# Laying the causal mask from ScalarE instead of multiplying it in, in a macaron layer with an mLSTM core

## The chip, the cores and the metric

The kernel runs on one core of one Trainium2 chip. The metric is the device time of one execution in microseconds (us); the time of the kernel before is the median of three runs.

## What is computed

The layer adds three things to an input of 4 sequences of 512 tokens by 128 channels: half of a top-1 mixture of experts (8 experts, 128 to 512 to 128), then an mLSTM block, then half of the same mixture again. The part that matters here is the mLSTM block. Its recurrence

```python
m_t = jnp.maximum(ft + m, it)
ie = jnp.exp(it - m_t)
fe = jnp.exp(ft - m_t + m)
c = fe[..., None, None] * c + ie[..., None, None] * jnp.einsum('bhd,bhe->bhde', vt, kt)
n = fe[..., None] * n + ie[..., None] * kt
num = jnp.einsum('bhde,bhe->bhd', c, qt)
den = jnp.maximum(jnp.sum(n * qt, -1, keepdims=True), 1.0)
```

over 512 steps and 8 heads of 64 is computed in chunks of 128 tokens. Inside a chunk the output is a masked product: scores (k times q, 128 by 128 for each head) are multiplied by decays exp(a_s - m_t) where s <= t, and by 0 elsewhere. What comes from before the chunk is the running state times q, scaled by a state decay exp(min - m_t). The zeros of the causal mask are made by adding -1e30 ahead of the exponential.

## The kernel before

Each engine has its own program, written out by hand, and semaphores tie them together. The mixture of experts runs first (`ffn(0)`), then four sequences (`sequence(b, last)`, three as iterations of a loop and the last unrolled), then `ffn(1)`. A sequence is four chunks (`chunk(b, c, last)`, c = 0 to 3). While the chunks of a sequence run, the projections of what comes next are woven in. After chunk 3 stand the q and k projections of the next sequence.

The eight banks of PSUM (the accumulator memory, 128 partitions by 512 fp32 each) have fixed uses. `PJ` is two banks, used in turn by the projections v, o, r (gate) and s (skip), so that each projection waits for the reader of the one two before it: project s waits for `take(.., "o")`, project r for `take(.., "v")`. `TR` holds transposes and state updates. `SB` is two banks for the scores of the even and of the odd heads. `NB_` is two banks for outputs. `DM` is one bank for the decays, used in a fixed order (`DM_USES`): carry and columns once for a sequence, then for every chunk even, odd and state. Each use waits until the use before it has been read (`dm_free`).

For a chunk TensorE does, in this order: decays of the even heads into DM, scores, project v of the next chunk, decays odd into DM, project o, a transpose of keys, state decays into DM, project r, project s, `from_state` (needs QS, the queries scaled by state decays), `to_state`, `values`. A group of decays is one identity matmul that writes the mask over the whole bank (128x512), and four 128x128 products accumulated on it. State decays have no mask.

ScalarE reads each group with four exponentials: `decays` (L796, even and odd, into DT, which shares its memory with the tile that the profile calls WVT), `state_decays` (L805, into E1, called E in the profile). Its order in a chunk is: decays even, `out_t` in chunk 3, take v, `out_t` in chunk 2 and `squares` in chunk 1, decays odd, `squares` in chunks 2 and 3, take o, state decays, take r, take s. VectorE multiplies scores by decays (`weigh`, L1994), makes QS from E1 (`scale_q`, L2001) and, after that, the chunk's head norm: `centre` ends in L2044, whose result `squares` (L816) reads.

In the profile every matmul but a few transposes is at L918, the helper, with "bank" as output: MASKB,IDB is the mask, M,SELQ a group of decays or state decays, SKIPB,ONESR the start of project s, CS,QS `from_state`. The timeline merges equal instructions (x4). For half of the 32 mask matmuls, those that open an even group, only the weight load is recorded and not the matmul.

Of the kernel before, what the change touches and what calls it, by code (L numbers as in the profile page):

```python
# [21 lines left out]
ACT = mybir.ActivationFunctionType  # L22
AX_X = mybir.AxisListType.X

P = 128
# [3 lines left out]
NC = 4  # L29
# [12 lines left out]
HD = 64  # L42
# [61 lines left out]
def macaron(nc, x, consts, colpack, rowpack, w_router, w1, w2, b2, wul, wult, wurt, wqt, wkt, wskt, wvt, wot,  # L104
# [9 lines left out]
    with ExitStack() as ctx:  # L114
        def sb(name, shape, dt=F32):
            return ctx.enter_context(nc.sbuf_tensor(name, shape, dt))

        def sem(name):
            return ctx.enter_context(nc.semaphore(name))
# [48 lines left out]
        IDB = sb("IDB", [P, P], BF16)  # L168
        MASKB = sb("MASKB", [P, 512], BF16)
# [3 lines left out]
        SELQ = sb("SELQ", [P, NC, H * P], BF16)  # L173
# [65 lines left out]
        M3 = sb("M3", [P, P], BF16)  # L239
# [12 lines left out]
        MINB = sb("MINB", [P, NC, NP_])  # L252
        E1 = sb("E1", [P, NP_, P])
# [75 lines left out]
        dm_full, dm_free, st_full, pt_ready = sem("dm_full"), sem("dm_free"), sem("st_full"), sem("pt_ready")  # L329
        hv_full, hv_read, cs_ready, qs_ready = sem("hv_full"), sem("hv_read"), sem("cs_ready"), sem("qs_ready")  # L330
        cen_ready, sq_ready, hvar_ready = sem("cen_ready"), sem("sq_ready"), sem("hvar_ready")
        hn_ready, outg_ready = sem("hn_ready"), sem("outg_ready")
        cs_copied = sem("cs_copied")


        PJ = bank[0:2]
        TR, DM = bank[2], bank[3]
        SB = bank[4:6]
# [26 lines left out]
            return pj_free[pj_bank(use)], b * (NPJ // 2) + pj_uses(b).index(use) // 2 + 2  # L365


        DM_USES = ["carry", "columns", *(f"{what}{c}" for c in range(NC) for what in ("even", "odd", "state"))]
        NDM = len(DM_USES)

        def dm_full_at(b, use):
            return dm_full, b * NDM + DM_USES.index(use) + 1

        def dm_read_at(b, use):
            return dm_free, b * NDM + DM_USES.index(use) + 2

# [229 lines left out]
        def _(act):  # L606
            a = nc.scalar
# [3 lines left out]
            def xn_channels(f, q):  # L611
                if f == 0:
                    act.wait_ge(xt_full[f], q + 1)
                    done = xt_copied[f]
                elif q < 3:
                    act.wait_ge(*pj_full_at(NB - 1, f"xt{q}"))
                    done = pj_free[q % 2]
                else:
                    act.wait_ge(xt_full[f], 1)
                    done = xt_copied[f]  # L620
                a.activation(XNT[:, q, :], bank[q % 2][:, :], ACT.Copy).then_inc(done, 1)
# [120 lines left out]
            def round_xc(b):  # L742

                act.wait_ge(xc_ready, b + 2)
                a.activation(XCH[:, :, :], XC[:, :, :], ACT.Copy).then_inc(xc_high, 1)
# [42 lines left out]
            def decays(b, c, hf):  # L788

                n = b * NC + c  # L790

                act.wait_ge(pt_ready, 2 * n + 1)
                act.wait_ge(*dm_full_at(b, f"{('even', 'odd')[hf]}{c}"))
                for m in range(4):
                    h = 2 * m + hf
                    ins = a.activation(DT[:, hf, m, :], DM[:, m * P:(m + 1) * P], ACT.Exp, bias=AC[:, c, h:h + 1])  # L796
                ins.then_inc(dm_free, 1)

            def state_decays(b, c):

                n = b * NC + c
                act.wait_ge(qs_ready, n + 1)
                act.wait_ge(*dm_full_at(b, f"state{c}"))
                for m in range(4):
                    ins = a.activation(E1[:, m, :], DM[:, m * P:(m + 1) * P], ACT.Exp, bias=MINB[:, c, m:m + 1])  # L805
                ins.then_inc(dm_free, 1)

            def first_state(b):

# [4 lines left out]
            def squares(b, c):  # L814
                act.wait_ge(cen_ready, b * NC + c + 1)
                a.activation(SQ[:, :, :], H2[:, :, :], ACT.Square).then_inc(sq_ready, 1)  # L816

            def out_t(b, c):

                act.wait_ge(*tr_full_at(b, f"o{c}"))  # L820
                a.activation(OUTT[:, :, :].rearrange("p m t -> p (m t)"), TR[:, :], ACT.Copy, scale=0.5)\
                    .then_inc(tr_free, 1)

            def chunk(b, c, last):
                nxt = (b, c + 1) if c < NC - 1 else None if last else (b + 1, 0)
                if c:
                    decays(b, c, 0)
                if c == 3:
                    out_t(b, 1)
                if last and c == 3:  # L830
                    xn_channels(1, 2)
                if nxt:
                    take(*nxt, "v")
                if c == 2:
                    out_t(b, 0)
                if c == 1:
                    squares(b, 0)
                decays(b, c, 1)
                if c > 1:
                    squares(b, c - 1)  # L840
                if nxt:
                    take(*nxt, "o")
                state_decays(b, c)
                if c == NC - 1 and not last:
                    round_xc(b + 1)
                    head_gates(b + 1)
                if nxt:
                    take(*nxt, "r")
                if c < NC - 1:
                    take(*nxt, "s")  # L850
                elif last:
                    layer_norm(1, 0)
                if c == 0:
                    first_state(b)
                if last and c == 2:
                    xn_channels(1, 0)
                    xn_channels(1, 1)
                if c == 1 and not last:
                    z_scaled(b + 1)
                if c == 2 and not last:  # L860
                    head_in(b + 1)
                    head_silu(b + 1)
# [51 lines left out]
        def _(pe):  # L914
            t_ = nc.tensor

            def mm(o, l, r, start=True, stop=True):
                return t_.matmul(o, l, r, start=start, stop=stop, skip_group_check=True)  # L918
# [178 lines left out]
            def dm_wait(b, use):  # L1097

                pe.wait_ge(dm_free, b * NDM + DM_USES.index(use) + 1)
                return DM  # L1100
# [106 lines left out]
            def decays(b, c, hf):  # L1207

                dm_wait(b, f"{('even', 'odd')[hf]}{c}")
                mm(DM[:, :], IDB[:, :], MASKB[:, :], True, False)  # L1210
                for m in range(4):
                    h = 2 * m + hf
                    ins = mm(DM[:, m * P:(m + 1) * P], SELQ[:, c, h * P:(h + 1) * P], M3[:, :], False, m == 3)
                ins.then_inc(dm_full, 1)

            def state_decays(b, c):

                dm_wait(b, f"state{c}")
                for m in range(4):

                    ins = mm(DM[:, m * P:(m + 1) * P], SELQ[:, c, 2 * m * P + HD:2 * m * P + HD + P], M3[:, :])
                ins.then_inc(dm_full, 1)

            def scores(b, c):

# [190 lines left out]
        def _(dve):  # L1416
# [580 lines left out]
            def scale_q(b, c):  # L1997

                n = b * NC + c
                dve.wait_ge(*dm_read_at(b, f"state{c}"))  # L2000
                v.tensor_tensor(QS[:, :, :], QT[:, :, c * P:(c + 1) * P], E1[:, :, :], ALU.mult).then_inc(qs_ready, 1)  # L2001

            def new_state(b, c):
# [279 lines left out]
```

## Time and profile before

| | |
|---|---|
| median of 3 runs | 427.73 us (426.88 to 428.43) |
| the profiled execution, its own time | 427.93 us |
| its span, first to last instruction | 425.7 us |
| mean granted TensorE clock | 0.953 of full speed; 1.00 from 125.5 to 345 us |
| sequence loop, one iteration | 57.7 us, from 125.5 us on |
| TensorE busy in the span | 378.5 us (89%) |
| VectorE busy | 320.2 us (75%) |
| ScalarE busy | 230.5 us (54%) |

The span lies 2.2 us below the execution's own time; that rest is start and end. Times in the rows are counted from the first instruction. "Busy" of TensorE counts pipelined matmuls, so 9 tenths busy can still hide waits of some tenths of a microsecond.

### The profile page before, as it was taken

How to read it: one execution, taken by the hardware profiler on the slowest of the kernel's cores; microseconds unless marked ns; L12 is line 12 of the kernel's file. 1: busy time of each engine (PE TensorE's matmuls, PEld its weight loads, DVE VectorE, ACT ScalarE, POOL GpSimd, SP SyncE). 2: the span in 40 equal slices, each digit the busy share in tenths (PEclk: the TensorE clock that was granted, in tenths of full speed). 3: DMA queues.
4: the chain of work that ended last, by engine and by line, in shares of the span. 5: the costliest groups of instructions: out<-in, count | busy, mean ns of one | idle time of the engine just before them, and what ended most of it. 6: DMA issues, size and time to landing. Idle time of an engine off the chain costs nothing.

```text
span 425.7 us, 11362 instructions
## 1 busy us (share of the span) xinstructions
PE 378.5 (89%) x3607; PEld 300.8 (71%) x3629; DVE 320.2 (75%) x1042; ACT 230.5 (54%) x607; POOL 124.2 (29%) x125
## 2 busy tenths in 40 slices
PE   8149999999999999999999999999989868779990
PEld 5123799964687777877878878778768734579990
DVE  4892677766728898878989788988788995567870
ACT  3641344442556767567684567665556912555550
POOL 5475145531001111103110121111031068434552
PEclk9657999999999999999999999999999969899997
DMA  6997122219999999989600000000001612323320
GB/s 199 370 418 227 46 78 62 68 57 217 181 171 174 174 170 162 175 170 173 153 5 0 0 0 0 0 0 0 2 2 42 235 62 87 113 82 92 97 68 0
DMA packets 57265, 46.10 MB, mean 108 GB/s; under 512 B 4112, under 2 KB 53906, under 8 KB 56722
## 3 DMA queue, kind: packets, MB, share of 16 engines
q1 hardware_dynamic: 53618, 37.84, 42.0%
q0 software_dynamic: 2752, 5.73, 3.9%
q10 hardware_dynamic: 864, 2.15, 1.6%
q8 instruction: 16, 0.26, 0.3%
q14 instruction: 15, 0.11, 0.1%
HBM read 17.99 MB, written 27.25 MB: 106 GB/s over the span
## 4 chain that ended last, share of the span: by engine, by line
PE 63%; DVE 12%; ACT 8%; issue 6%; DMA 3%; POOL 3%; another core or an unknown queue 1%; SPq 0%; DVEq 0%; POOLq 0%; ACTq 0%
PE bank L918 59%; ACT WVT L796 4%; POOL slots L521 2%; DVE ST L1450 1%; PE bank L1288 1%; ACT E L805 1%; PE bank L1055 1%; DMA XN<-slots 1%; ACT W1R L816 1%; DMA slots<-XN,POS 1%; DVE QS L2001 1%; ACT XNT L736 1%; DMA QKT<-by_token 1%; DMA by_token<-YB,IDX 1%
## 5 line engine op out<-in xcount | busy, mean ns | idle before, releaser
L569 POOL TENSOR_TENSOR HS<-HS,MHALF 128x8 f32<-128x8 f32 x16 | 26.4, 1647 | 130.9 <-DVE HS L2051 130.9
L918 PE MATMUL bank<-XBT,W1R 128*128 128x128 f32 x368 | 50.1, 280 | 0.5 <-ACT XBT L691 0.4
L918 PE MATMUL bank<-W,HT 128*128 x368 | 49.0, 276 | 0.7 <-issue 0.7
L918 PEld LDWEIGHTS bank<-XBT,W1R 128*128 128x128 f32 x368 | 45.3, 194 | 1.7 <-ACT XBT L691 1.4
L918 PEld LDWEIGHTS bank<-W,HT 128*128 128x128 f32 x368 | 44.8, 192 | 1.2 <-issue 0.8
L698 ACT ACTIVATE HT<-bank,W1R 128x128 f32<-128x128 f32 x115 | 34.8, 366 | 16.2 <-PE bank L918 12.5
L796 ACT ACTIVATE WVT<-bank,AC 128x128 f32<-128x128 f32 x128 | 36.6, 376 | 11.8 <-PE bank L918 11.7
L521 POOL DMA_INDIRECT slots<-XN,POS x32 | 32.6, 1018 | 19.4 <-issue 13.0
L918 PE MATMUL bank<-MASKB,IDB 128*128 128x512 bf16 x130 | 35.4, 398 | 3.0 <-POOL HS L569 1.2
L760 ACT ACTIVATE QKT<-bank,COLS 128x512 f32<-128x512 f32 x32 | 22.0, 687 | 29.0 <-PE bank L918 29.0
L550 POOL DMA_INDIRECT by_token<-YB,IDX x23 | 22.0, 958 | 30.3 <-DVE YB L1713 29.9
L553 POOL DMA_INDIRECT out<-YB,IDX x23 | 22.7, 985 | 24.4 <-DVE YB L1716 16.8
L918 PEld LDWEIGHTS bank<-MASKB,IDB 128*128 128x128 bf16 x151 | 14.5, 101 | 20.8 <-issue 3.3
L1994 DVE TENSOR_TENSOR WOT<-bank,WVT 128x512 f32<-128x512 f32 x32 | 21.9, 685 | 8.8 <-ACT WVT L796 8.5
L1706 DVE TENSOR_SCALAR HT<-bank,W1R 128x128 f32<-128x128 f32 x69 | 22.0, 347 | 8.4 <-PE bank L918 6.5
L691 ACT ACTIVATE XBT<-bank 128x128 f32<-128x128 f32 x46 | 12.6, 277 | 26.8 <-PE bank L1055 13.4
L1679 DVE COPY OUT<-B 128x128 f32 x41 | 10.3, 251 | 20.5 <-issue 17.5
L561 POOL TENSOR_TENSOR LA<-LA,MHALF 128x4 f32<-128x4 f32 x4 | 4.1, 1015 | 68.1 <-DVE LA L1869 68.1
L918 PE MATMUL bank<-M,SELQ 128*128 128x128 bf16 x192 | 18.7, 220 | 5.7 <-ACT WVT L796 3.3
L918 PEld LDWEIGHTS bank<-M,SELQ 128*128 128x128 bf16 x192 | 13.8, 98 | 10.2 <-ACT WVT L796 6.1
L1680 DVE COPY W1R<-W 128x516 f32 x41 | 18.7, 455 | 0.3 <-issue 0.3
L918 PE MATMUL bank<-QKT 64*128 64x128 f32 x256 | 18.6, 285 | 0.0
(363 smaller groups left out, 972.4 us busy)
## 6 DMA issues: line engine op xcount, KB each, us to landing
slots<-FILL SPq DMA_DIRECT2D x74, 258.0 KB, 7.9
W<-w SPq DMA_DIRECT2D x2, 2048.0 KB, 10.6
XN<-slots SPq DMA_DIRECT2D x23, 129.0 KB
W<-w SPq DMA_DIRECT2D x1, 2064.0 KB
slots<-QKT SPq DMA_DIRECT2D x1, 1483.5 KB, 6.2
XB<-slots SPq DMA_DIRECT2D x23, 64.5 KB
X<-x SPq DMA_DIRECT2D x4, 256.0 KB, 5.3
QKT<-by_token SPq DMA_DIRECT2D x4, 256.0 KB, 4.0
```

The costliest lines, as they stand in the source:

```text
L521: g.indirect_dma_start(out=slots[f], out_offset=bass.IndirectOffsetOnAxis(ap=POS[:, t:t + 1], axis=0), in_=XN[f][:, t, :], in_offset=None) ...
L550: ins = g.indirect_dma_start(out=by_token, out_offset=number, in_=YB[:, j, :], in_offset=None)
L553: ins = g.indirect_dma_start(out=out, out_offset=number, in_=YB[:, j, :], in_offset=None, bounds_check=NT * P - 1, oob_is_err=False)
L569: g.tensor_tensor(HS[:, 3, :], HS[:, 2, :], MHALF[:, 0:H], ALU.pow).then_inc(roots_ready, 1)
L691: a.activation(XBT[:, j % 2, :], bank[j % 2][:, 0:P], ACT.Copy).then_inc(xbt_copied[f], 1)
L698: ins = a.activation(HT[:, j % 2, c, :], bank[2 + j % 2][:, c * P:(c + 1) * P], ACT.Relu, bias=W1R[:, j % 2, F + c:F + c + 1])
L760: a.activation(QKT[:, m, :], PJ[i][:, :], ACT.Identity, bias=col("bq", m)).then_inc(pj_free[i], 1)
L796: ins = a.activation(DT[:, hf, m, :], DM[:, m * P:(m + 1) * P], ACT.Exp, bias=AC[:, c, h:h + 1])
L918: return t_.matmul(o, l, r, start=start, stop=stop, skip_group_check=True)
L1680: v.tensor_copy(W1R[:, j % 2, :], W1[:, e, :]).then_inc(w1_copied[f], 1)
L1706: ins = v.tensor_scalar(HT[:, j % 2, c, :], bank[4 + j % 2][:, at:at + P], W1R[:, j % 2, F + c:F + c + 1], 0.0, ALU.add, ALU.max)
L1994: v.tensor_tensor(PT[:, hf, :, :].rearrange("p m t -> p (m t)"), SB[hf][:, :], DT[:, hf, :, :].rearrange("p m t -> p (m t)"), ALU.mult).th ...
```

## The change

Seven of the eight groups of decays of a sequence (four chunks, even and odd) lose their mask matmul. Only the first one, even of chunk 0, keeps it. In place of the matmul ScalarE copies the mask MASKB into DM, as soon as its own four exponentials have read the group before, and the four products accumulate on that. Decays odd of chunk 3 is the last group of a sequence, and no mask is laid after it. State decays leave DM: they go into `SB[0]`, the bank of the even scores, once VectorE has weighed these (`pt_ready`), with semaphores of their own (`sd_full`, `e1_ready`).

```diff
-        DM_USES = ["carry", "columns", *(f"{what}{c}" for c in range(NC) for what in ("even", "odd", "state"))]
+        DM_USES = ["carry", "columns", *(f"{what}{c}" for c in range(NC) for what in ("even", "odd"))]
         NDM = len(DM_USES)
+        LAST_DECAYS = (NC - 1, 1)
...
-                ins.then_inc(dm_free, 1)
+                ins.then_inc(dm_free if (c, hf) == LAST_DECAYS else decays_read, 1)
+
+            def lay_mask(b, c, hf):
+                if (c, hf) == LAST_DECAYS:
+                    return
+                act.wait_ge(decays_read, b * (2 * NC - 1) + 2 * c + hf + 1)
+                a.activation(DM[:, :], MASKB[:, :], ACT.Copy).then_inc(dm_free, 1)
...
-                act.wait_ge(*dm_full_at(b, f"state{c}"))
+                act.wait_ge(sd_full, n + 1)
                 for m in range(4):
-                    ins = a.activation(E1[:, m, :], DM[:, m * P:(m + 1) * P], ACT.Exp, bias=MINB[:, c, m:m + 1])
-                ins.then_inc(dm_free, 1)
+                    ins = a.activation(E1[:, m, :], SB[0][:, m * P:(m + 1) * P], ACT.Exp, bias=MINB[:, c, m:m + 1])
+                ins.then_inc(e1_ready, 1)
...
                 if c:
                     decays(b, c, 0)
+                lay_mask(b, c, 0)
                 if c == 3:
                     out_t(b, 1)
...
                 decays(b, c, 1)
                 if c > 1:
                     squares(b, c - 1)
+                lay_mask(b, c, 1)
                 if nxt:
                     take(*nxt, "o")
                 state_decays(b, c)
...
-                mm(DM[:, :], IDB[:, :], MASKB[:, :], True, False)
+                if (c, hf) == (0, 0):
+                    mm(DM[:, :], IDB[:, :], MASKB[:, :], True, False)
...
-                dm_wait(b, f"state{c}")
+                pe.wait_ge(pt_ready, 2 * (b * NC + c) + 2)
                 for m in range(4):
-                    ins = mm(DM[:, m * P:(m + 1) * P], SELQ[:, c, 2 * m * P + HD:2 * m * P + HD + P], M3[:, :])
-                ins.then_inc(dm_full, 1)
+                    ins = mm(SB[0][:, m * P:(m + 1) * P], SELQ[:, c, 2 * m * P + HD:2 * m * P + HD + P], M3[:, :])
+                ins.then_inc(sd_full, 1)
...
-                dve.wait_ge(*dm_read_at(b, f"state{c}"))
+                dve.wait_ge(e1_ready, n + 1)
```

## Rows read from the trace of the kernel before

**Rows 1.** The page, part 1: busy time of each engine

```profile
PE 378.5 (89%) x3607; PEld 300.8 (71%) x3629; DVE 320.2 (75%) x1042; ACT 230.5 (54%) x607; POOL 124.2 (29%) x125
```

**Rows 2.** Windows, one loop iteration: length, busy of PE, PEld, DVE, ACT, POOL; clock

```profile
183.30:241.02 57.72, 56.16 (x624) 45.46 (x628) 49.77 (x127) 38.05 (x96) 8.57 (x6) 1.00 0.41 84
```

**Rows 3.** Waits from 125.5 to 340 us: total, times, longest

```profile
PEld bank L918 <- ACT WVT L796: 8.7, 16, 1.4
```

**Rows 4.** The chain that ended last, chunk 3: start, length, what

```profile
221.74 0.70 DVE QS L2001
222.48 7.96 PE bank L918 x86
```

**Rows 5.** Timeline of TensorE, chunks 0 to 2: start, length, what, idle before

```profile
190.21 0.84 PE L918 MATMUL bank<-CS,QS 64*128 64x1 f32 x28
...
194.97 0.39 PE L918 MATMUL bank<-MASKB,IDB 128*128 128x512 bf16 x1
195.20 0.39 PE L918 MATMUL bank<-M,SELQ 128*128 128x128 bf16 x4
...
197.38 0.40 PE L918 MATMUL bank<-M,SELQ 128*128 128x128 bf16 x4 [0.59 <-ACT WVT L796]
...
198.37 0.39 PE L918 MATMUL bank<-SKIPB,ONESR 65*128 65x512 f32 x1
...
200.07 0.95 PE L918 MATMUL bank<-CS,QS 64*128 64x65 f32 x28
...
210.12 0.95 PE L918 MATMUL bank<-CS,QS 64*128 64x65 f32 x28
```

**Rows 6.** Timeline of ScalarE, chunks 1, 2 and 3

```profile
195.66 0.62 ACT L816 ACTIVATE W1R<-W1R 128x512 f32<-128x512 f32 x1
196.19 1.14 ACT L796 ACTIVATE WVT<-bank,AC 128x128 f32<-128x128 f32 x4
197.19 0.62 ACT L781 ACTIVATE XN<-bank 128x512 f32<-128x512 f32 x1
197.81 1.15 ACT L805 ACTIVATE E<-bank,MINB 128x128 f32<-128x128 f32 x4
...
207.11 0.67 ACT L816 ACTIVATE W1R<-W1R 128x512 f32<-128x512 f32 x1
...
208.10 1.19 ACT L805 ACTIVATE E<-bank,MINB 128x128 f32<-128x128 f32 x4
...
216.52 1.13 ACT L796 ACTIVATE WVT<-bank,AC 128x128 f32<-128x128 f32 x4
...
220.57 1.14 ACT L805 ACTIVATE E<-bank,MINB 128x128 f32<-128x128 f32 x4
```

**Rows 7.** Timeline of VectorE, chunks 0, 1 and 2

```profile
189.13 0.69 DVE L2001 TENSOR_TENSOR QS<-QKT,E 128x512 f32<-128x512 f32 x1 [0.34 <-ACT E L805]
...
198.99 0.69 DVE L2001 TENSOR_TENSOR QS<-QKT,E 128x512 f32<-128x512 f32 x1 [0.58 <-ACT E L805]
...
206.20 0.69 DVE L2044 TENSOR_TENSOR W1R<-W1R,HS 128x512 f32<-128x512 f32 x1
...
209.33 0.69 DVE L2001 TENSOR_TENSOR QS<-QKT,E 128x512 f32<-128x512 f32 x1
```

**Rows 8.** Groups by form, ScalarE over 128x512: count, busy, mean ns

```profile
L760 ACT ACTIVATE QKT<-bank,COLS 128x512 f32<-128x512 f32 x32 | 22.0, 687 | 29.0 <-PE bank L918 29.0
L821 ACT ACTIVATE OUTT<-bank 128x512 f32<-128x512 f32 x16 | 9.6, 598 | 13.2 <-PE bank L1288 13.1
```

**Rows 9.** Timeline of ScalarE, a wait on its own semaphore between these two

```profile
239.66 0.21 ACT L770 ACTIVATE DEC<-bank 128x16 f32<-128x16 f32 x1
239.91 0.60 ACT L821 ACTIVATE OUTT<-bank 128x512 f32<-128x512 f32 x1
```

**Rows 10.** Timeline of TensorE in the last sequence, chunks 1 and 3

```profile
314.02 0.40 PE L918 MATMUL bank<-M,SELQ 128*128 128x128 bf16 x4 [1.22 <-ACT WVT L796]
...
334.91 0.40 PE L918 MATMUL bank<-M,SELQ 128*128 128x128 bf16 x4 [0.30 <-ACT WVT L796]
```

More of the change, by code:

```diff
@@ L332, in macaron @@
         hn_ready, outg_ready = sem("hn_ready"), sem("outg_ready")
-        cs_copied = sem("cs_copied")
+        cs_copied, decays_read = sem("cs_copied"), sem("decays_read")
+        sd_full, e1_ready = sem("sd_full"), sem("e1_ready")
         PJ = bank[0:2]
```

## The prediction, made before the changed kernel ran

> **What bounds the kernel now.** I read the busy times first. TensorE is busy 378.5 us of the span, VectorE 320.2, ScalarE 230.5 [rows 1]. That makes TensorE the engine to relieve and ScalarE the one with room, and in one iteration of the sequence loop it looks the same: 56.16, 49.77 and 38.05 us busy of 57.72, at a full clock [rows 2]. The second look is at waits. Between 125.5 and 340 us TensorE's weight loads stood 8.7 us behind the decays' exponentials, in 16 waits [rows 3]: state decays want DM, and ScalarE has not yet read the odd group out of it. An example is chunk 1 of the second sequence, with 0.59 us of idle ahead of the state decays at 197.38 [rows 5].
>
> The third look, the chain, spoils the picture. Once in every sequence it leaves TensorE: in chunk 3 it comes to `from_state` at 222.48 through QS at 221.74 [rows 4], and QS waited for ScalarE's E1 at 220.57 [rows 6]. In the timeline ScalarE has no idle from the even exponentials at 216.52 to E1 at 220.57. So a busy share of 66% in the iteration (38.05 / 57.72) hides stretches in which ScalarE's order of work decides. I therefore follow each chunk through, and compare its `from_state`, which needs both project s (so take o) and QS (so E1).
>
> **What is removed.** A mask matmul takes 0.23 us from its start to that of the next, 194.97 to 195.20 [rows 5]. I use 0.22 for one. There are 7 in a sequence, 1.5 us, and 28 in all, 6.2 us, which is all the matmuls can give. Their weight loads go with them. The state decays no longer wait for the odd exponentials. They wait for the weighing of the even scores, which VectorE mostly finishes before.
>
> **What is added.** Seven ScalarE copies of 128x512 from a bf16 tile into PSUM for each sequence, each behind its own four exponentials. No row has ScalarE writing PSUM. The nearest rows are 128x512 with no bias at 598 ns, PSUM to SBUF, and with a bias 687 ns [rows 8]. Back to back such a copy holds the engine for less than its length: 195.66 to 196.19 is 0.53 us for a row of 0.62, and elsewhere 0.48 to 0.50. I take 0.60 long and s = 0.50 us of engine time. The bounds are s = 0.40 below (an overlap of 0.2 in place of the 0.1 seen) and s = 0.69 above, the longer row with no overlap. A bound of nothing is excluded: 512 columns go through the same engine.
>
> The copy also waits for the last of the four exponentials to end, where the next instruction used to overlap it. Four exponentials are 1.14 us long, but the next instruction starts 1.00 after them (196.19 to 197.19, rows 6), and a wait of ScalarE on its own semaphore ends 0.04 us after the instruction waited for (239.66 + 0.21 to 239.91 [rows 9]). That makes 0.14 + 0.04 + 0.50 = 0.68 us of delay for what stands behind the copy, and 0.50 where `squares` lies between and covers the drain.
>
> No row here shows what it does to a copy that it goes to PSUM. On this the Trainium skill's page "ScalarE: Activation LUTs" (section "Step-by-step: what each stage is for") holds that ScalarE writes PSUM faster than SBUF. It gives no figure there; by it s would lie toward the lower bound, and with s = 0.40 the sum below would be 3.9 us in place of 4.9.
>
> **Chunk by chunk, second sequence.** All changes are against the time before. One engine's idle absorbs a delay, and only what reaches `from_state` is passed on.
>
> Chunk 0. The odd group comes 0.22 earlier, the copy delays take o and E1, and the sum for E1 is +0.30. QS, before at 189.13, ends at 189.13 + 0.30 + 0.69 = 190.12. With 0.05 to TensorE that is 190.17, against `from_state` at 190.21 [rows 5, 7]. TensorE gains the matmul and loses it waiting: shift 0.
>
> Chunk 1. `squares` needs the centring of VectorE, which has been delayed by 0.3 with QS, and stays at 195.66. The odd exponentials stay at 196.19 and end at 197.33. The copy goes from 197.37, take o starts at 197.87 in place of 197.19 (+0.68) and is 0.62 long, so project s starts at 198.54 in place of 198.37. E1 follows take o by 0.48, at 198.35 in place of 197.81 (+0.54; it waited for TensorE before, and the state decays are now early). QS moves from 198.99 to 199.53 and ends at 200.22, so `from_state` starts at 200.27 in place of 200.07: +0.20 [rows 5 to 7]. The 0.59 us of TensorE idle is gone at the state decays, and comes back a few matmuls later ahead of project s.
>
> Chunk 2. TensorE wins back 0.22 with the even mask, so the scores and exponentials keep their times. VectorE doesn't: from QS in chunk 1 to its centring at 206.20 it runs without a gap. So that moves by 0.54 to 206.74, and ends 207.43. `squares` starts at 207.47 in place of 207.11 (+0.36). With the copy's 0.50, E1 starts at 208.10 + 0.86 = 208.96, ends 210.13, QS starts 210.16 (209.33 before) and ends 210.85, `from_state` starts at 210.90 in place of 210.12: +0.78 [rows 5 to 7].
>
> Chunk 3. The next sequence's input conversions follow `from_state`, TensorE and ScalarE in turn, and bring +0.78 to the even exponentials at 216.52. From there ScalarE has no gap up to E1, and the copy after the even group adds 0.68. E1 moves by 1.46 from 220.57, and QS and `from_state` with it. What follows is bound by TensorE (7.96 us in one piece, rows 4) and keeps the delay.
>
> With s left open the three copies on this path are odd 1, odd 2 and even 3, and the iteration grows by about 3s - 0.05 us. For s = 0.50 that is 1.45, with 1.15 and 2.0 at the bounds. All seven mask matmuls and both kinds of TensorE waits are then priced at what they give: next to nothing, since each is followed by a wait for take o or QS.
>
> **The last sequence** has no next one to convert. Its VectorE work in chunk 0 is longer, and TensorE waited 1.22 us for the odd exponentials in chunk 1 and 0.30 us in chunk 3 [rows 10]; the second of these lay on the path to E1, and is gone. Followed in the same way, it gives +0.4 at chunk 1, +0.6 at chunk 2, and in chunk 3 the copy's 0.68 less what the earlier state decays return, which leaves +0.6. Bounds: 0.3, and 1.4 if it behaves like the others.
>
> **The sum.** 3 x 1.45 + 0.6 = 4.95 us. On the profiled execution's 427.93 this is 432.9; the median lies 0.2 lower, so 432.7 us, 1.2% slower. Bounds: 3 x 1.15 + 0.3 = 3.7 (431.4), and 3 x 2.0 + 1.4 = 7.4 (435.1).
>
> **Rivals.** A change under 0.3%, 1.3 us, is about what can't be told from none here.
>
> First, on the other side: the copies fall into ScalarE's idle time, 57.72 - 38.05 = 19.7 us of an iteration, against 3.5 us of copies. Then chunks 1 and 2 keep take o and E1 where they are, and TensorE runs 1.5 us shorter in each sequence: -6.2 us, 421.5. The single price that decides it is s: the path gains only if a copy delays take o by less than 0.02 us. Even then chunk 3, bound by ScalarE, would give back most, leaving about 0.3 for each sequence: 426.5. What speaks for it is the share of idle; against it, the idle lies ahead of take v and take s and not between the odd exponentials and E1. Chance 6 in 100.
>
> Second, no change: the time of project s and QS has slack that I don't see, say 0.4 us in each of three chunks, so that only chunk 3's 0.3 or so is left: +1, 428.7. The rows have 0.0 to 0.1 us of slack in chunk 0 and about 0.1 in chunk 2. Chance 9 in 100.
>
> Third, half of it: the last sequence takes nothing, and s is below 0.35: about 3 x 0.95 = +2.9 or less, 430.6 and below, down to the bound of no change. Chance 10 in 100.
>
> Fourth, dearer: ScalarE writing PSUM costs 0.69 with no overlap, or the wait on its own semaphore costs more than 0.04. +7.4 us and above, 435.1. Chance 7 in 100.
>
> The forecast has the rest, 68 in 100, between 431 and 435. The range 430.0 to 434.9 leaves out the first two, the lower end of the third and the fourth. Slower: 68 + 10 + 7 = 85; same 9; faster 6.
>
> **What would show it.** In the changed profile the rows of mask matmuls from 125 to 340 us fall from 32 weight loads to 4, and a ScalarE group bank<-MASKB 128x512 appears with 28 instructions near 600 ns. The wait of TensorE's loads on L796 goes, in its place stand waits on take o (L781, tile XN) ahead of SKIPB,ONESR in chunks 1 and 2, and on QS (L2001) ahead of CS,QS. One loop iteration is 59.2 us in place of 57.7. TensorE's busy time falls by some 6 us while the span grows, and its clock stays at 1.00 in the loop. I am wrong if take o starts less than 0.4 us later behind the odd exponentials, if `from_state` of chunk 2 is not later within its iteration, or if chunk 3's even exponentials are followed by idle ScalarE time.

## The result and the profile after

The changed kernel takes 434.67 us (median of 4 runs, 433.94 to 435.74) against 427.86 us (426.88 to 428.43, 4 runs) for the kernel before on the same chip: a ratio of 1.0185, interval 1.0157 to 1.0212. It is slower. The medians differ by 6.8 us (434.67 / 427.86 = 1.0159), while the ratio with its interval stands for 7.9 us; which of the two is nearer, four runs of each kernel don't tell. The forecast was 432.7 us, with a range of 430.0 to 434.9. The median lies inside that range by 0.2 us; the ratio lies above its upper end, 434.9 / 427.73 = 1.0168. The profiled execution took 433.95 us with a span of 432.0 us, 6.3 us longer than the span before.

The page, part 1, of the changed kernel:

```profile
PE 377.3 (87%) x3600; PEld 295.4 (68%) x3601; DVE 321.0 (74%) x1042; ACT 246.1 (57%) x635; POOL 124.2 (29%) x125
```

ScalarE gained 28 instructions and 15.6 us of busy time, TensorE lost 1.2 us, and the span grew [rows 1]. The recorded weight loads fell from 3629 to 3601, which are the 28 mask matmuls. The recorded matmuls fell by 7 only, since some matmul records are missing in either trace, so TensorE's busy time does not measure what was removed. The window of one loop iteration says the same, at a full clock as before, with 59.78 us in place of 57.72 [rows 2]:

```profile
185.82:245.60 59.78, 56.27 (x623) 44.47 (x621) 50.07 (x127) 42.14 (x103) 8.57 (x6) 1.00 0.26 59
```

The copies, as the group of instructions on the tile MASKB (shortest/median/longest in nanoseconds, then the first and the last start in us):

```profile
L807 ACT ACTIVATE bank<-MASKB x28: 582/602/603, 127.5 to 339.6; 128x512 f32<-128x512 bf16 x28
```

And the waits of the changed kernel from 125.5 to 347 us (in total, times, longest):

```profile
PEld bank L930 <- ACT XN L783: 8.6, 12, 1.5
...
PEld bank L930 <- ACT bank L807: 8.1, 9, 1.8
...
PEld bank L930 <- DVE WOT L2007: 4.7, 8, 1.2
```

The 8.7 us behind the decays' exponentials [rows 3] are gone. In their place stand 8.6 us behind take o (XN, L783; 0.8 before), 8.1 behind the copy and 4.7 behind the weighing. The waits on QS stay as they were, 5.4 us before and 5.5 after. The idle of TensorE in chunk 1 shows how one wait became the other. These are lines from the timeline of TensorE of the changed kernel, chunks 0 to 3 of the second sequence:

```profile
192.79 0.84 PE L930 MATMUL bank<-CS,QS 64*128 64x1 f32 x28
...
201.13 0.50 PE L930 MATMUL bank<-SKIPB,ONESR 65*128 65x512 f32 x1 [1.09 <-ACT XN L783]
201.47 0.40 PE L930 MATMUL bank<-WSKH,XCH 128*128 128x512 f32 x1
...
202.94 0.95 PE L930 MATMUL bank<-CS,QS 64*128 64x65 f32 x28
...
213.79 0.95 PE L930 MATMUL bank<-CS,QS 64*128 64x65 f32 x28
...
226.80 0.95 PE L930 MATMUL bank<-CS,QS 64*128 64x65 f32 x28 [0.30 <-DVE QS L2014]
```

The 0.59 us ahead of the state decays [rows 5] has become 1.09 us ahead of project s. ScalarE shows why. Its timeline in the same chunks 1, 2 and 3:

```profile
198.27 0.63 ACT L826 ACTIVATE W1R<-W1R 128x512 f32<-128x512 f32 x1
198.80 1.12 ACT L798 ACTIVATE WVT<-bank,AC 128x128 f32<-128x128 f32 x4
199.96 0.60 ACT L807 ACTIVATE bank<-MASKB 128x512 f32<-128x512 bf16 x1
200.50 0.58 ACT L783 ACTIVATE XN<-bank 128x512 f32<-128x512 f32 x1
200.97 1.13 ACT L815 ACTIVATE E<-bank,MINB 128x128 f32<-128x128 f32 x4
...
210.28 0.63 ACT L826 ACTIVATE W1R<-W1R 128x512 f32<-128x512 f32 x1 [0.37 <-DVE W1R L2057]
210.81 0.58 ACT L807 ACTIVATE bank<-MASKB 128x512 f32<-128x512 bf16 x1
...
211.81 1.13 ACT L815 ACTIVATE E<-bank,MINB 128x128 f32<-128x128 f32 x4
...
220.17 1.12 ACT L798 ACTIVATE WVT<-bank,AC 128x128 f32<-128x128 f32 x4
221.33 0.60 ACT L807 ACTIVATE bank<-MASKB 128x512 f32<-128x512 bf16 x1
...
224.88 1.14 ACT L815 ACTIVATE E<-bank,MINB 128x128 f32<-128x128 f32 x4
```

From the start of the odd exponentials to that of take o it was 196.19 to 197.19, 1.00 us [rows 6], and is 198.80 to 200.50, 1.70 us. In chunk 3, even exponentials to E1 was 216.52 to 220.57, 4.05 us [rows 6], and is 4.71 us. The forecast had +0.68 for each; they are +0.70 and +0.66.

**Where the time went.** I place the two traces on the first even exponentials of each sequence: 126.70, 183.78, 241.50 and 299.25 us before, and 126.30, 186.29, 246.08 and 305.89 us after. The first sequence is 2.91 us longer, the second 2.07, the third 2.06. From the last of these starts to the router's first step behind the sequences (VectorE's cast POS) it is 43.96 before (to 343.21) and 44.54 after (to 350.43), +0.58. Together +7.62. The loop starts 0.40 us earlier, and from POS to the end of the span it is 82.49 us before and 81.57 after, 0.92 shorter; the change touches neither. That makes 7.62 - 0.40 - 0.92 = 6.30, the growth of the span. So the place to explain is 7.62 against the forecast's 4.95.

Aligned to the start of the second sequence, `from_state` of chunks 0 to 3 is later by 0.07, 0.36, 1.16 and 1.81 us, where the forecast had 0, 0.20, 0.78 and 1.46. The next sequence starts 2.07 later, where the forecast kept 1.46. The mechanism is the one forecast. Some tenths are missing, and a part appears behind chunk 3, where the forecast saw TensorE as the bound and nothing to lose.

The chain that ended last shows that part. Changed kernel, 240 to 245 us:

```profile
240.67 0.70 DVE W1R L2071
241.38 0.02 issue
241.40 0.70 DVE W1R L2072
242.10 0.03 issue
242.13 0.04 DVEq L2073
242.17 0.04 issue
242.21 0.70 DVE W1R L2074
242.92 0.02 issue
242.94 0.70 DVE OUT L2110
243.64 0.05 issue
243.69 0.66 PE bank L1301 x4
```

Kernel before, the same place:

```profile
238.91 0.22 PE bank L1179 x2
239.13 0.14 PE bank L918 x2
239.28 0.49 PE bank L1288 x4
239.77 1.09 PE bank L918 x16
```

Before, TensorE reached these four transposes (K,OUT) without a wait. After, the chain comes to them through VectorE's head norm and gated output, and between L2072 and L2074 it passes through a piece of VectorE's queue (its sequencer), DVEq, at L2073. L2073 is a wait, `dve.wait_ge(*pj_read_at(b, f"s{c}"))`. From the end of one instruction to the start of the next there are 0.11 us here, where the others of this head norm have 0.02.

### The profile page after: what moved, and what is told of

The parts are those of the page before. It is cut to its first block, busy times and chain, and to the rows that moved or that the text cites. A ratio compares the mean times of both kernels' runs of the same rounds, so it can differ in the third digit from the quotient of the medians.

```text
span 432.0 us, 11424 instructions
## 1 busy us (share of the span) xinstructions
PE 377.3 (87%) x3600; PEld 295.4 (68%) x3601; DVE 321.0 (74%) x1042; ACT 246.1 (57%) x635; POOL 124.2 (29%) x125
## 4 chain that ended last, share of the span: by engine, by line
issue 40%; PE 27%; DVE 17%; POOL 8%; ACT 3%; DMA 2%; another core or an unknown queue 1%; DVEq 0%; POOLq 0%; SPq 0%; ACTq 0%
PE bank L930 25%; POOL HS L571 5%; POOL slots L523 2%; DVE ST L1463 1%; PE bank L1067 1%; ACT WVT L798 1%; ACT E L815 1%; POOL LA L565 1%; DVE W1R L2072 1%; DMA QKT<-by_token 1%; DVE W1R L2071 1%; DVE SA L1876 1%; PE bank L1301 1%; DVE W1R L2046 1%
## 5 line engine op out<-in xcount | busy, mean ns | idle before, releaser
L930 PE MATMUL bank<-MASKB,IDB 128*128 128x512 bf16 x123 | 31.7, 397 | 2.5 <-POOL HS L571 1.9
L930 PEld LDWEIGHTS bank<-MASKB,IDB 128*128 128x128 bf16 x123 | 11.7, 101 | 16.7 <-POOL HS L571 2.4
L930 PEld LDWEIGHTS bank<-M,SELQ 128*128 128x128 bf16 x192 | 12.2, 98 | 15.6 <-ACT bank L807 8.1
L930 PE MATMUL bank<-WDT,OUTT 128*128 128x128 f32 x128 | 18.6, 291 | 0.4
```

## What the missing 2.7 us might be

A wait names a semaphore and the count that it must have reached, its threshold. Inside the loop the thresholds are register values, `b * 14 + constant` for `DM` before, and 14 a sequence for `TR` and for the readers of each bank of `PJ` too. With the change `dm_full` and `dm_free` count 10 in a sequence and `decays_read` counts 7. In the built programs register arithmetic grows from 85 to 93 instructions on VectorE, 47 to 56 on TensorE and 53 to 60 on ScalarE. The traces have the same growth, 24, 27 and 21 more such instructions executed in three iterations. The register theory: the different multipliers cost arithmetic between waits, and this is on the path in the head norm. The first rival: the copies cost more than their own length, through contention on the bank or a slow writing of PSUM. The second: moving the state decays makes TensorE wait for VectorE's weighing.

All comparisons are of one loop iteration, `from_state` of chunk 0 to the same of the next sequence, iterations 1 and 2 of the profile, one profiled execution for each kernel. Whole times of one kernel scatter by 2 us or more, an iteration much less: v5h and v5i, which differ in one flag, have 57.31 and 57.30 in the first and 57.09 and 57.04 in the second. I compare the second. The four steps are those between the `from_state` of chunks 0, 1, 2, 3 and the next 0, in the second sequence; they add up to the second iteration.

| kernel | median us (runs) | ratio to before, interval | iterations | steps |
|---|---|---|---|---|
| before | 427.86 (4) | | 57.75, 57.73 | 9.86 10.05 12.36 25.46 |
| changed | 434.67 (4) | 1.0185 [1.0157, 1.0212] | 60.06, 59.78 | 10.15 10.85 13.01 25.77 |
| pad14 | 430.55 (6) | 1.0114 [1.0075, 1.0153] | 59.66, 59.36 | 10.15 10.69 13.03 25.49 |
| before15 | 426.33 (12) | 1.0001 [0.9966, 1.0035] | 58.02, 58.01 | 9.86 10.06 12.37 25.72 |
| hidden5 | 424.08 (12) | 0.9963 [0.9931, 0.9996] | 58.36, 57.86 | 9.36 10.64 12.37 25.49 |
| v7 | 431.47 (2) | 1.0143 [1.0090, 1.0196] | 59.74, 60.30 | 10.94 10.71 13.11 25.54 |
| v4 | 428.74 (10) | 1.0021 [0.9994, 1.0049] | 58.14, 58.01 | 9.56 10.53 12.37 25.55 |
| v0 | 427.35 (10) | 0.9974 [0.9943, 1.0005] | 57.81, 57.56 | 9.46 10.52 12.36 25.22 |
| v5h | 424.29 (9) | 0.9922 [0.9892, 0.9952] | 57.31, 57.09 | 9.27 10.20 12.39 25.23 |
| v5i | 421.70 (7) | 0.9908 [0.9876, 0.9940] | 57.30, 57.04 | 9.27 10.19 12.36 25.22 |
| lay2b | 445.35 (2) | 1.0395 [1.0346, 1.0443] | 62.62, 62.32 | 10.68 11.39 13.54 26.71 |

pad14, before15 and hidden5 ran on one chip beside a median of 425.38 us for the kernel before; v4, v0, v5h and lay2b on a second beside 428.11; v7 and v5i on a third occasion beside 425.03. So whole times from different occasions can't be compared directly; compare the ratios.

## Experiment pad14: the changed kernel, with every bank's count back at 14

```diff
+        DM_STEP = {"columns": 5}
+        NDM = sum(DM_STEP.get(u, 1) for u in DM_USES)      # 14
...
-                act.wait_ge(decays_read, b * (2 * NC - 1) + 2 * c + hf + 1)
+                act.wait_ge(decays_read, b * 2 * (2 * NC - 1) + 2 * (2 * c + hf + 1))
```

The signals of "columns" count 5, those of `decays_read` 2. Copies, order and waits stay. Expected:

> The changed kernel with the same work, but its wait thresholds count 14 for each sequence again, as they did before the change (columns count 5, each reading of decays counts 2), so that they share registers with the thresholds of the projection and transpose banks. Theory A (part of the excess over the forecast is register arithmetic that now stands between waits on VectorE, about 0.08 us at each of several places of the chain behind QS): a loop iteration falls from 59.8 to about 59.4 us, VectorE's chain from QS of chunk 3 to the last gated output falls from 16.9 to 16.6 us, and the whole is 1 to 1.5 us below the changed kernel, 433 to 433.5 us. Rival B (the excess is only TensorE's slower restart after its new waits, and where the copies stand): nothing changes, 434.7 us.

Measured: 59.36 us in the second iteration against 59.78, so 0.42 us of an iteration is the thresholds, 0.28 of it in the fourth step and 0.16 in the second. Register arithmetic on VectorE and TensorE is down to 87 and 48 instructions (ScalarE keeps 59 of 60). What is left of the change makes 59.36 - 57.73 = 1.63 us. Over the whole time pad14's ratio is 1.0114 against the changed kernel's 1.0185, which is 3 us where 1 to 1.5 were expected; the two kernels ran on different occasions, and I rest on the iteration. On VectorE's timeline of pad14 the pair that L2073 separated is closed:

```profile
228.90 0.69 DVE L2081 TENSOR_TENSOR W1R<-W1R,ROWS 128x512 f32<-128x512 f32 x1
229.63 0.69 DVE L2083 TENSOR_TENSOR W1R<-W1R,SK 128x512 f32<-128x512 f32 x1
```

Start to start that is 0.73 us. In the changed kernel it is 0.81:

```profile
231.14 0.69 DVE L2072 TENSOR_TENSOR W1R<-W1R,ROWS 128x512 f32<-128x512 f32 x1
231.95 0.69 DVE L2074 TENSOR_TENSOR W1R<-W1R,SK 128x512 f32<-128x512 f32 x1
```

## Experiment before15: the kernel before, with DM counting 15

```diff
+        DM_STEP = {"columns": 2}
+        NDM = sum(DM_STEP.get(u, 1) for u in DM_USES)      # 15
```

No copy is laid and no work differs from the kernel before, only a threshold's multiplier. Register arithmetic goes from 85, 47 and 53 instructions (VectorE, TensorE, ScalarE) to 96, 59 and 58. Expected:

> The kernel before with one edit: the count of DM uses is 15 for each sequence in place of 14 (columns count 2), no work is added. Theory A (register arithmetic): VectorE's chain behind QS of chunk 3 grows from 16.6 to about 16.9 us, and as the transposes of the last gated output follow it within 0.1 us, each iteration grows by 0.2 to 0.3 us: 428.3 to 429.0 us. Rival B: the thresholds' registers cost nothing, 427.9 us.

Measured: 58.01 us against 57.73, +0.28 in an iteration, nearly all of it in the fourth step (25.72 against 25.46). The gap between the two VectorE instructions opened as in the changed kernel, to 0.82 us:

```profile
225.44 0.69 DVE L2065 TENSOR_TENSOR W1R<-W1R,ROWS 128x512 f32<-128x512 f32 x1
226.26 0.69 DVE L2067 TENSOR_TENSOR W1R<-W1R,SK 128x512 f32<-128x512 f32 x1
```

From the start of QS in chunk 3 to the end of its gated output it is 17.32 us before (221.74 to 239.06), 17.58 in before15, 17.58 in the changed kernel and 17.31 in pad14. These are the last gated output before, and QS and the last gated output of the changed kernel:

```profile
238.37 0.69 DVE L2097 TENSOR_TENSOR OUT<-W1R,GR 128x512 f32<-128x512 f32 x1
```

```profile
226.05 0.69 DVE L2014 TENSOR_TENSOR QS<-QKT,E 128x512 f32<-128x512 f32 x1 [0.38 <-ACT E L815]
...
242.94 0.69 DVE L2110 TENSOR_TENSOR OUT<-W1R,GR 128x512 f32<-128x512 f32 x1
```

The same holds for every kernel of the table: 17.31 or 17.32 in the seven in which every count is 14 (before, pad14, v7, v4, v0, v5h, v5i), and 17.58 or 17.59 in the four in which one is not (changed, before15, hidden5, lay2b). The register theory holds for this part. The other 0.16 that pad14 won, in the second step, has no such second witness: before15 has more register arithmetic on TensorE than the changed kernel and loses nothing there. Over the whole time, 0.28 in each of three iterations is 0.2%, and the ratio 1.0001 [0.9966, 1.0035] can't resolve it.

## Experiments v7, v4 and v0: which copies cost

A family with 14 as the multiplier of every threshold, and a table of the groups behind whose exponentials ScalarE lays a mask; groups without one keep the mask matmul. v7 has all seven, v4 only four (it leaves out the copies after odd 1, odd 2 and even 3, which the forecast called on the path), v0 none, so that v0 is the move of the state decays to `SB[0]` alone.

```diff
+        LAYS = [(0, 0), (0, 1), (1, 0), (1, 1), (2, 0), (2, 1), (3, 0)]   # v7
+        LAYS = [(0, 0), (0, 1), (1, 0), (2, 0)]                           # v4
+        LAYS = []                                                         # v0
...
-                if (c, hf) == (0, 0):
+                if ((c, 0) if hf else (c - 1, 1)) not in LAYS:
                     mm(DM[:, :], IDB[:, :], MASKB[:, :], True, False)
```

In all three the weighing of VectorE waits for the exponentials again (`decays_read`), and not for the copy behind them, as the change has it.

> The changed kernel with all seven copies and thresholds of 14, and in addition VectorE's weighing waits for the exponentials and not for the copy behind them, which it does in the changed kernel. Theory A (that wait lies off the path): 59.3 to 59.45 us an iteration, as with thresholds of 14 alone (59.36). Rival G (weighing behind the copy is part of the loss, above all in chunk 2, where the state decays wait for it): 59.1 or less.

> The changed kernel's state decays in the bank of the even scores, and four of its seven copies: those behind even 0, odd 0, even 1 and even 2. The three that the forecast put on the path (behind odd 1, odd 2 and even 3) are matmuls again. Thresholds count 14 for a sequence and VectorE's weighing waits for the exponentials and not for the copy, so that VectorE's program has the same register instructions as before the change. Theory A (these three copies are the loss): a loop iteration is back at 57.7 us, between 57.5 and 57.9, against 59.4 with all seven and thresholds of 14. Rival C (every copy costs): 58.5 us or more. Rival F (the moved state decays are the loss, through the wait for VectorE's weighing): stays near 59.

> One part alone: state decays in the bank of the even scores, every mask a matmul as before the change, register instructions as before. Theory A: TensorE's waits for the odd exponentials go in chunks 0 and 1, chunk 1's from_state is about 0.5 us earlier, and chunk 2 gives most of it back, where the state decays now wait for VectorE's weighing of the even scores: an iteration of 57.5 us, against 57.7 before, and the whole 0.5 to 1 us below it. Rival F (moving the state decays costs by itself): 58 us or more an iteration.

Measured: v7's second iteration holds one stall of 0.9 us behind chunk 0's `from_state` that its others don't have; its third takes 59.52 us against pad14's third of 59.47. That is just above the 59.3 to 59.45 expected, and far from rival G's 59.1. So releasing VectorE with the copy in place of the exponentials cost nothing that shows. v4: 58.01 against pad14's 59.36, so the three copies cost 1.35 us of an iteration: 0.59 in the first step (odd 1), 0.66 in the third (even 3), and 0.16 in the second (odd 2), where v4 meets another wait, that of v0 below. In the first and third iteration the same difference is 1.52 and 1.53. The third step can be read from the `from_state` of chunks 2 and 3, in v4 and then in pad14:

```profile
211.52 0.95 PE L954 MATMUL bank<-CS,QS 64*128 64x65 f32 x28
223.89 0.95 PE L954 MATMUL bank<-CS,QS 64*128 64x65 f32 x28 [0.30 <-DVE QS L2054]
```

```profile
211.53 0.95 PE L939 MATMUL bank<-CS,QS 64*128 64x65 f32 x28
224.56 0.95 PE L939 MATMUL bank<-CS,QS 64*128 64x65 f32 x28 [0.30 <-DVE QS L2023]
```

v4's 58.01 is 0.1 above the upper end of what was expected. The copies of chunk 0 aren't free either: the fourth step is 25.55 with them and 25.22 in v0. v0: 57.56, 0.17 below the kernel before. So pad14's 1.63 us are made up of -0.17 for the move of the state decays, +0.45 for v4's four copies and +1.35 for the three others. The move of the state decays alone wins 0.40 in the first step and 0.24 in the fourth, and gives back 0.47 in the second, where they wait for VectorE. From the timeline of TensorE in v0, chunk 2 (the second rival, in that one chunk):

```profile
209.65 0.40 PE L954 MATMUL bank<-M,SELQ 128*128 128x128 bf16 x4 [0.30 <-DVE WOT L2047]
```

In the changed kernel this wait is 0.81 us, with the state decays at 210.90, but take o stands later still (211.34) and E1 follows it, so there it is not what holds the chunk.

## Experiment lay2b: every copy twice

```diff
+                a.activation(SPARE[:, :], MASKB[:, :], ACT.Copy)
                 a.activation(DM[:, :], MASKB[:, :], ACT.Copy).then_inc(dm_free, 1)
```

> The changed kernel with a second copy of the mask ahead of each of the seven, into a spare tile that nothing reads. Theory A (three copies of a sequence are on the path, one more in the first sequence's chunk 0): 0.5 to 0.55 us more for each makes an iteration 1.5 to 2.0 us longer than the 59.8 of the changed kernel, 61.3 to 61.8. Rival C (all seven on the path): 63.3 or more. Rival D (not the length of the copies but the waits around them): below 60.3.

Measured: 62.32 against 59.78 us, +2.54 in an iteration. That is above the 1.5 to 2.0 of theory A and below rival C's 3.5; neither range was met. The steps rise by 0.53, 0.54, 0.53 and 0.94: once a copy is twice as long, those of chunk 0 reach the path as well. The group rows, the added copy to SBUF and the one to PSUM:

```profile
L808 ACT ACTIVATE SPARE<-MASKB x28: 614/631/663, 127.6 to 349.9; 128x512 bf16<-128x512 bf16 x28
L809 ACT ACTIVATE bank<-MASKB x28: 582/582/636, 128.2 to 350.5; 128x512 f32<-128x512 bf16 x28
```

One more copy on the path costs 0.53 us, which is the time from a copy's start to that of the next instruction (199.96 to 200.50 in the changed kernel's rows above). The added copy goes to SBUF, so this run prices a place in ScalarE's order, and not a write into the bank; a form with both copies into DM (lay2) gave no result, as its two writes of one bank had no semaphore between them. Against the first rival speak the rows: the copies into the bank are 582 to 603 ns long in the changed kernel, and the next instruction follows one by 0.53 to 0.54 us, as it does behind a copy to SBUF. In lay2b, side by side, the copy into PSUM is shorter than the one into SBUF, 582 against 631 ns (their outputs differ in type, too); by the Trainium skill's page "ScalarE: Activation LUTs" (section "Step-by-step: what each stage is for"), that writing to PSUM is the faster, this trace agrees, by 49 ns. In v5i below the copies into PSUM take 601 to 681 ns, and the advantage doesn't show.

## Experiments hidden5, v5h and v5i: the copies where ScalarE is idle

Five groups keep a copy. The copy after an odd group moves behind take r, into the time in which ScalarE waited for take s. Those after even 0 and even 3 are given back to TensorE. In hidden5 all state decays are in `SB[0]`.

```diff
+        LAYS = [(0, 1), (1, 0), (1, 1), (2, 0), (2, 1)]
...
-                lay_mask(b, c, 1)
                 if nxt:
                     take(*nxt, "o")
                 state_decays(b, c)
                 if nxt:
                     take(*nxt, "r")
+                lay_mask(b, c, 1)
```

> State decays in the bank of the even scores as in the change, but only five masks are laid, where ScalarE has idle time: those behind even groups of chunks 1 and 2, and those behind odd groups of chunks 0, 1 and 2, which are made later, after take r. The other two are matmuls again. VectorE's weighing and TensorE wait for the exponentials and not for the copy. Theory A (the change lost only by where its copies stand): all waits for take o go, from_state in chunks 1 and 2 is 0.3 to 0.5 us earlier than in the kernel before, and the whole is 0.5 to 1.5 us below it, 426.3 to 427.3 us. Rival E (chunk 3, bound by ScalarE and VectorE, and VectorE's chain give nothing back): 427.9 us, as before. Rival D (copies into PSUM or the new bank for state decays cost by themselves): above 429.

Measured: 57.86 us in the second iteration, 0.13 above the kernel before. Against it, the first step fell by 0.50 and the second rose by 0.59, as in v0: the state decays wait for VectorE's weighing. So `from_state` is 0.50 earlier in chunk 1, as expected, and 0.09 later in chunk 2, where 0.3 to 0.5 earlier was expected; TensorE still waits 0.40 us for take o in chunk 1. The fourth step has a copy after odd 0 and counts that are not 14. The ratio of whole times is 0.9963, interval 0.9931 to 0.9996, some 1.6 us below the kernel before; the iterations don't show it, and where it comes from stays open. Timeline of TensorE in hidden5, chunk 2:

```profile
206.83 0.40 PE L939 MATMUL bank<-M,SELQ 128*128 128x128 bf16 x4 [0.48 <-DVE WOT L2024]
```

So v5h leaves the state decays of chunk 2 in DM, behind the odd exponentials as before, and has all multipliers at 14.

```diff
+        STATE_IN_SB = (0, 1, 3)
...
-                pe.wait_ge(pt_ready, 2 * (b * NC + c) + 2)
+                if c in STATE_IN_SB:
+                    pe.wait_ge(pt_ready, 2 * (b * NC + c) + 2)
+                else:
+                    pe.wait_ge(*decays_read_at(b, c, 1))
```

> Five copies where ScalarE has idle time (behind even 1 and even 2 in place, behind odd 0, 1 and 2 after take r), state decays in the bank of the even scores in chunks 0, 1 and 3, but in DM in chunk 2, where VectorE's weighing is late, and thresholds of 14. Theory A (each loss has its own place, and this avoids all of them: the copies on the path, the wait for weighing in chunk 2, the register instructions): an iteration of 56.9 to 57.3 us, against 57.7 before and 57.9 with five copies alone; the whole 1.5 to 3 us below the kernel before. Rival E (chunk 3 and VectorE's chain give nothing back): 57.7 us.

v5h leaves out a part of the computation: in each sequence three quarters of the mask of even 3 are missing. It takes 57.09 us an iteration and 0.9922 [0.9892, 0.9952] of the kernel before's whole time, some 0.3 us more of a gain than expected, and its second step is 0.44 shorter than hidden5's, where the wait for the weighing stood. v5i has that mask whole. Its one edit is the start flag of chunk 2's state decays, set only on the first of four products:

```diff
                     ins = mm((SB[0] if c in STATE_IN_SB else DM)[:, m * P:(m + 1) * P], SELQ[:, c, 2 * m * P + HD:2 * m * P + HD + P], M3[:, :],
+                             c in STATE_IN_SB or m == 0)
```

> As v5h, with one difference: of chunk 2's four state-decay products into DM only the first starts the accumulation anew, so that the mask laid on that bank afterwards is added to by the next even group over all 512 columns. Theory A: the same work in the same order, so the same time as v5h, an iteration of 57.0 to 57.2 us against 57.73 before, and the whole 2 to 4 us below the kernel before. Rival: v5h was faster only because three quarters of one mask were lost; then this one is slower than it by 0.2 us an iteration or more.

Measured: 57.04 us, as v5h, so that the missing mask was not what made v5h fast, and 0.69 below the kernel before in an iteration; over the whole time 0.9908 [0.9876, 0.9940], so v5i is faster than the kernel before by 0.9%, and than the changed kernel by more, with 20 copies where the change has 28. ScalarE's timeline in v5i, chunk 1: take r, the copy and take s back to back, where the changed kernel has 0.46 us of idle between take r (201.97) and take s (203.05).

```profile
201.78 0.66 ACT L804 ACTIVATE RTH<-bank 128x512 f32<-128x512 f32 x1
202.25 0.67 ACT L829 ACTIVATE bank<-MASKB 128x512 f32<-128x512 bf16 x1
202.89 0.60 ACT L807 ACTIVATE SK<-bank 128x512 f32<-128x512 f32 x1
```

## Why the prediction was right in kind and short in size

**What bounds.** Right. Neither 6 us of matmuls nor 8.7 us of TensorE's waits were worth much by themselves: moving the state decays alone (v0) gives 0.17 us of an iteration. The path in chunks 1 to 3 goes through ScalarE's order of work. The rival on the other side (the copies fall into idle time) fell with v4 and pad14: three copies cost 1.35 to 1.53 us of an iteration. It holds for a copy that is put where the idle time is, as in v5i.

**The price of a copy.** Right: 0.60 us long as forecast; 0.53 to 0.54 of engine time where I took 0.50; a wait on its own semaphore as forecast. The dearer rival, 0.69 or more, fell with these rows. The sentence that s would lie toward the lower bound of 0.40, since a write to PSUM is faster, did not come true: s came out above 0.50. Its 3.9 us is also a little low: with s = 0.40 the terms of the sum give 3 x 1.15 + 0.6 = 4.05.

**Chunk 0.** The forecast kept its `from_state` where it was, and pad14's fourth step is indeed 25.49 against 25.46. But this is two things that cancel and not nothing: moving the state decays gives 0.24 (v0), and the copies of chunk 0 take it back (0.33 from v0 to v4).

**The last sequence.** +0.6 forecast, +0.58 measured.

**The failed step** is the term "3 x 1.45" of the sum. It measured 2.91 + 2.07 + 2.06 = 7.04 in place of 4.35. Three things were missing.

First, about 0.4 in each iteration of register arithmetic between waits, a term that the forecast did not have. It is shown by pad14 (-0.42) and, for the 0.28 behind chunk 3, by before15. The forecast said of the stretch behind `from_state` of chunk 3 that it "is bound by TensorE and keeps the delay". It had no slack against VectorE's head norm, and that became longer by 0.26.

Second, about 0.2 in each iteration remains between pad14's 1.63 and the forecast's 1.45. Most of it lies in chunks 1 and 2. In the changed kernel the first matmul of project s is recorded 0.50 us long where it had to wait for take o, and the next starts 0.34 later (201.13 to 201.47). Before, it was 0.39 long [rows 5] and the next started 0.23 later (198.37 to 198.60). Project s starts in the longer way in chunks 0 to 2 of this sequence, so its end, and `from_state` with it, can come 0.11 later in each; before, it started so in none of them. This is read from the rows; no experiment isolated it, and the 0.2 stays unproven.

Third, I took the three iterations as alike. In the first sequence ScalarE had next to no room in chunk 0. From the even exponentials to the odd ones it was 1.85 us (126.70 to 128.55) with 0.22 idle, and is 2.26 (126.30 to 128.56), since the first copy lies between. In the second sequence the same stretch had 0.80 us of idle, and did not grow (2.54 before, 2.33 after). In the changed kernel the first sequence's first `from_state` is 0.67 later against its start (0.07 in the second), and the sequence has grown by 0.84 more than the second. The timeline of before had these rows, and the forecast did not use them.

The sum with these is 4.95 + 3 x 0.41 + 3 x 0.2 + 0.84 = 7.6 us. That it meets the 7.62 is no proof, since the 0.2 and the 0.84 are what was left over; 0.41 and 1.35 were measured apart. Of the 7.62 the profiled span shows 6.3, as the rest of that execution was 1.3 shorter.

**The signs named.** Weight loads of the mask in the sequences fell to 4, the copy group has 28 instructions of 602 ns, the waits moved to XN as named, the clock stayed at 1.00. None of the three signs of being wrong appeared: take o starts 0.70 later, `from_state` of chunk 2 is later by 1.16, and ScalarE stays without idle behind chunk 3's even exponentials up to E1. The waits on QS did not grow, and those behind the copy itself (8.1 us) were not named. One loop iteration is 59.8 and not 59.2, and TensorE's busy time fell by 1.2 and not by 6 us.

## What to carry to other kernels

An engine's busy share says nothing about where added work may stand: write down the engine's order and put it in front of an instruction that waits anyway. The copy after odd 1 costs some 0.6 us ahead of take o (v4) and nothing that shows behind take r (hidden5, v5i). When a change moves semaphores, the counts in a loop are part of the change: keep them at one common multiplier, or price the arithmetic between waits. And when relieving one wait, look at the other releaser: the state decays left the exponentials' bank only to wait for VectorE in one chunk of four.

## What I had not expected of the chip

A threshold's multiplier alone costs time: 0.08 to 0.09 us at the place above where register arithmetic falls between two instructions that otherwise follow closely (0.73 to 0.81 and 0.82 us), 0.28 us of an iteration in before15.

In v5h ScalarE writes the whole bank for even 3, and three quarters of that mask have no effect in the output; in v5i, with the start flag on the first of the four products of the state decays alone, they have. The layer worked out with the mask of even 3 left out for heads 0, 2 and 4, the first three quarters, deviates by 0.0825 of its size, which is v5h's deviation to six digits. For head 6, the fourth quarter, the mask changes nothing in this output, so the two kernels say nothing about it. Both kernels take the same time (57.09 and 57.04 us an iteration). The Trainium skill's page "PSUM — Partial Sum Buffer" (section "The four PSUM rules") has a reason: a start flag clears the accumulation marks of the whole bank, and a later product without it overwrites where the mark is clear. By it the last of four products leaves only its own quarter marked. The two kernels agree with that for the first three quarters.
